# Sixteen resident weight units and twelve head rotations whose sums are made by accumulating transfers

## The chip, the cores and the metric

One NeuronCore of a Trainium2 chip runs the whole kernel in one launch. The metric is the device time of that core in microseconds (us). The engines are TensorE (PE in the rows, its weight loads PEld), VectorE (DVE), ScalarE (ACT), GpSimd (POOL) and SyncE (SP), which here only issues transfers.

## What is computed

One decoder layer on x (8 batches of 100 tokens, 1024 wide) with a context of 8 x 722 rows:

```python
# retention, 8 heads, key width 128, value width 256
q, k, v, g = x @ Wq, x @ Wk, x @ Wv, x @ Wg          # q and k get a rotary turn:
x1, x2 = halves of the 128 wide head
rope = concatenate([x1 * cos - x2 * sin, x2 * cos + x1 * sin])
scores = (q * scale) @ k.T * decay                   # causal
o = scores @ v;  o = o * rsqrt(mean(o*o) + eps) * weight * silu(g)
x = layernorm(x + o @ Wo)
# attention over context and tokens, 16 query heads, 4 key/value heads of 128
q, k = rope(rmsnorm(...)), keys and values of the context in front
x = layernorm(x + softmax(q @ k.T) @ v @ wo)         # wo: 2048 x 1024
# feed-forward of width 4096
x = layernorm(x + (silu(x @ gate) * (x @ up)) @ down)
```

All of it is in float32 accuracy. A product a @ b is made as three products of rounded parts, high x high, high x low, low x high, where low = value - high.

## The kernel before

**Layout.** Activations stand with 128 channels on the partitions and the 800 tokens (NT) along the free axis, 1024 channels as KT = 8 tiles. A *weight unit* is 128 output channels of a 1024 x 1024 piece, 128 x 1024 numbers (512 KB). SP loads two units at a time (1024 KB) from HBM into one of the two slots of `RAW`, in the order in which `_pack_weights` laid them out. ACT copies a unit into its rounded high part (`WH`), DVE subtracts it and so makes the low part (`WL`), and TensorE multiplies. `WH` and `WL` hold two units each. A slot of `RAW` is loaded again once the low parts of its two units are made (`weight_stream`, waiting for `c.w_lo`). Every engine runs its own list of instructions in the order of the code; semaphores (`wait_ge`, `then_inc`) tie them.

**Retention (`phase_retention`).** Heads 1 to 6 are alike (`head(i)`, 72.6 us each): three blocks of seven products by a Strassen scheme (`product`), the output projection of the head before (`project_output`, L2362 to L2364), then `scores`, `turn`. On DVE `combine` (L2031) adds partial products into the block's result; product 3 of a block waits for its first one (`u2`). Q and k come out of block 0 in `QKR`. DVE turns them: `rotate_cos` (L2073) writes T1 = QKR * cos, `rotate_sin` (L2078) writes T2 from the other half of the partitions in two instructions of 64 partitions, `rotate_sum` (L2086) makes T1 - T2, ACT copies the high part (`rotated_hi`, L1764), DVE makes the low part (`rotated_lo`, L2090). `add_output` (L2100) adds a projected tile to the residual `R`; tile n of the projection waits for `add_output(n - 2)`.

**Between retention and attention.** The last two heads' projection runs by halves of 400 tokens (HALF), so that the first layernorm (`HalfNorm`: mean, centre L1452, squares L1433, variance, root, refine L1458 to L1463, normal L1470) of one half lies beside the products of the other. DVE also makes here the low parts of the four value units (`values_lo`, L2114, into `VW`).

**The tail (`phase_tail`).** The attention output projection has 16 units. The second eight (from `U_WO1`) are used by halves: all eight units on tokens 0 to 399, then all eight on tokens 400 to 799. Before, they stand twice in the packed weights, are loaded twice and split twice (`split_hi` L93, `split_lo` L99). The feed-forward goes in four chunks. The down projection of the last chunk (`down_by_halves`, L3687 to L3689) has the same pattern: eight units on 400 tokens, then the same eight loaded and split again (`unit_hi` L3775, `unit_lo` L3996) for the other 400, with the last layernorm (`final`) between and behind them. Its variance of half 0 is taken ahead of unit 12 (`take_variance`, L1420). After the last product come the mean, eight centrings, the last squares, two folds (L1355), variance, root, three refining steps and eight `normal`s, and SP stores the result in pairs of tiles.

**GpSimd** sets some constants and is otherwise free.

Of the kernel before, what the change touches and what calls it, by code (L numbers as in the profile page):

```python
# [21 lines left out]
F32 = mybir.dt.float32  # L22
F32R = mybir.dt.float32r
# [39 lines left out]
U_FFN = U_WO1 + 16  # L63
U_END = U_FFN + 24 * CHUNKS + 8
PRODUCTS = 7
ENTRIES = 8 * PRODUCTS + 2 * KT
PAIRS = U_END // 2

# [87 lines left out]
def phase_context(c, nc, sem):  # L156

    with ExitStack() as ctx:
# [1121 lines left out]
        done.k_stored, done.v_stored = k_stored, v_stored  # L1280
        done.K_STORED = [k_stored_by(GROUPS) for _ in range(2)]
# [16 lines left out]
class HalfNorm:  # L1298

    def __init__(self, c, sem_of, name, mean_banks, var_banks, SUM, SQ, Y, Z,  # L1300
                 folded=(0, 0)):
# [4 lines left out]
        self.folded = folded  # L1306
# [5 lines left out]
    @staticmethod  # L1312
    def half(ap, h):
        return ap[:, h * HALF:(h + 1) * HALF]

    @staticmethod
    def tile(x, k, h):
        return x[:, k, h * HALF:(h + 1) * HALF]

    def mean_bank(self, h):  # L1320
        return self.c.PS[:, self.MEAN_BANK[h], 0:HALF]

    def var_bank(self, h):
        return self.c.PS[:, self.VAR_BANK[h], 0:HALF]
# [23 lines left out]
    def add_last_four(self, dve):  # L1348

        for n, (a, b) in enumerate(((4, 5), (6, 7), (4, 6))):  # L1350
# [4 lines left out]
            dve.tensor_tensor(self.SQ[:, a, :], self.SQ[:, a, :], self.SQ[:, b, :],  # L1355
                              ALU.add).then_inc(self.sq_sum, 1)

    def take_last_variance(self, pe):
        for k in range(5):
# [4 lines left out]
            mm = pe.matmul(self.var_bank(1), self.ones[:], self.SQ[:, k, :], start=(k == 0),  # L1364
# [3 lines left out]
    def add_squares(self, dve, h, ks):  # L1368

        for k in ks:  # L1370
# [3 lines left out]
            dve.tensor_tensor(self.SQ[:, 0, :], self.SQ[:, 0, :], self.SQ[:, k, :],  # L1374
                              ALU.add).then_inc(self.sq_sum, 1)

    def add_pairs(self, dve, h):

        for n, (a, b) in enumerate(((0, 1), (2, 3), (4, 5), (6, 7), (0, 2), (4, 6), (0, 4))):
# [4 lines left out]
            dve.tensor_tensor(self.SQ[:, a, :], self.SQ[:, a, :], self.SQ[:, b, :],  # L1384
# [8 lines left out]
    def add_fours(self, dve, h):  # L1393

        adds = ((0, 1), (2, 3), (0, 2), (4, 5), (6, 7), (4, 6))
        for n, (a, b) in enumerate(adds[:self.folded[h]]):
# [4 lines left out]
            dve.tensor_tensor(self.SQ[:, a, :], self.SQ[:, a, :], self.SQ[:, b, :],  # L1401
                              ALU.add).then_inc(self.sq_sum, 1)

    def take_variance_of_fours(self, pe, h):
        parts = (4, 5, 6, 7, 0) if self.folded[h] == 3 else (0, 4)
        for k in parts:
# [6 lines left out]
            mm = pe.matmul(self.var_bank(h), self.ones[:], self.SQ[:, k, :],  # L1413
# [3 lines left out]
    def take_variance(self, pe, h):  # L1417
        if self.folded[h]:
            pe.wait_ge(self.sq_sum, self.folds(h + 1))
            pe.matmul(self.var_bank(h), self.ones[:], self.SQ[:, 0, :], start=True,  # L1420
                      stop=True).then_inc(self.sq_used, 1)
            return
        for k in range(KT):
            pe.wait_ge(self.squared, KT * h + k + 1)
            pe.matmul(self.var_bank(h), self.ones[:], self.SQ[:, k, :], start=(k == 0),
                      stop=(k == KT - 1)).then_inc(self.sq_used, 1)

    def squares(self, act, h, ks):
        for k in ks:
# [3 lines left out]
            act.activation(self.SQ[:, k, :], self.tile(self.c.R, k, h),  # L1433
# [75 lines left out]
def phase_retention(c, nc, sem, before, norm):  # L1509


    with ExitStack() as ctx:
# [33 lines left out]
                 "s_raw", "s_masked", "s_hi", "s_lo", "gated", "o_raw", "o_sq", "o_products", "o_ln",  # L1546
                 "o_rs", "o_normed", "o_hi", "o_lo", "wo_raw", "r_added",
                 "v_kept", "v_turned", "wo_last", "o_scaled", "o_back")
        (turned, roped, qk_hi, qk_lo, v_hi, v_lo, s_raw, s_masked, s_hi, s_lo,
         gated, o_raw, o_sq, o_products, o_ln, o_rs, o_normed, o_hi, o_lo, wo_raw,  # L1550
         r_added, v_kept, v_turned, wo_last, o_scaled, o_back) = (sem("r_" + n) for n in names)

        f_hi, F_HI = before.k_sq, 8 * GROUPS
# [130 lines left out]

        def scalar(act):
# [269 lines left out]
        def vector(dve):  # L1955
# [119 lines left out]
            def rotate_sin(i, n, half):  # L2075

                lo, hi = 64 * half, 64 - 64 * half
                ins = dve.tensor_tensor(  # L2078
                    batches(T2[lo:lo + 64]), batches(QKR[hi:hi + 64, n, :]),
                    c.SIN[hi:hi + 64].unsqueeze(1).broadcast_to([64, B, T]), ALU.mult)  # L2080
                if half:
                    ins.then_inc(turned, 1)
# [28 lines left out]
            def values_lo(v):  # L2111
                u = U_V + v
                dve.wait_ge(c.w_hi, u + 1)
                dve.tensor_tensor(c.VW[:, v, 1, :], raw_unit(c, u), c.VW[:, v, 0, :].bitcast(F32),  # L2114
                                  ALU.subtract).then_inc(c.w_lo, 1)

# [16 lines left out]
            def mask_scores(i):  # L2133
                dve.wait_ge(s_raw, i + 1)
# [55 lines left out]
            def head(i):  # L2190
# [38 lines left out]
                product_lo(i, 1, 4)  # L2229
                mix(i, 1, 3)  # L2230
                combine(i, 1, "u2")
                rotate_sin(i, 0, 0)
                product_lo(i, 1, 5)
                rotate_sin(i, 0, 1)
# [3 lines left out]
                rotate_sum(i, 0)  # L2238
                output_entry_lo(i, 0)
                rotated_lo(i, 0)  # L2240
                rotate_cos(i, 1)
                output_entry_lo(i, 1)
                rotate_sin(i, 1, 0)
                combine(i, 1, "c21")
                output_entry_lo(i, 2)
                rotate_sin(i, 1, 1)
# [3 lines left out]
                rotate_sum(i, 1)  # L2250
                output_entry_lo(i, 3)
                add_output(1, i)
                rotated_lo(i, 1)
                add_output(2, i)
                mix(i, 2, 0)
# [77 lines left out]
            for n in range(KT):  # L2333
                add_last(0, n)
                if n == 2 or n == 5:
                    values_lo(n // 3)
# [7 lines left out]
            values_lo(2)  # L2344
            values_lo(3)
# [278 lines left out]
        return sync, scalar, vector, tensor, r_added  # L2624


def phase_heads(c, nc, sem, before, norm, r_added):
# [4 lines left out]
    with ExitStack() as ctx:  # L2632
# [217 lines left out]
        def vector(dve, first_queries, first_maxima):  # L2850
# [30 lines left out]
            copy_value(0)  # L2881
            split_lo(c, dve, U_V + 4)
# [461 lines left out]
def phase_tail(c, nc, sem_of, attention):  # L3344
# [4 lines left out]
    with ExitStack() as ctx:  # L3349
# [5 lines left out]
        def below(words, *tiles):  # L3355

            with ExitStack() as room:
                out = []
                for n, (gap, *shape) in enumerate(tiles):
                    if gap:  # L3360
                        room.enter_context(nc.sbuf_tensor(f"{words}_gap{n}", [P, gap], F32))
                    out.append(room.enter_context(nc.sbuf_tensor(f"{words}{n}", [P, *shape], F32)))
# [4 lines left out]
        f_sum, f_y, f_z, f_sq, ones = below("t_fn", (2 * FLAT + 2 * SIDE, NT), (0, NT), (0, NT),  # L3367
                                            (0, KT, HALF), (0, P))
# [1020 lines left out]
```

## Time and profile before

| | us |
|---|---|
| median of 3 runs | 2636.43 (2636.38 to 2636.45) |
| the profiled execution | 2636.99 |
| its span, first to last instruction | 2635.2 |
| TensorE busy | 2598.2 |
| VectorE busy | 1858.9 |
| ScalarE busy | 1214.2 |

The span is what the rows below divide up; 1.8 us lie around it. A row of a timeline gives start and duration in us; matmuls overlap, so that the distance from one start to the next is what one costs. A bracket at the end of a row is the idle time of the engine ahead of it and what ended it.

### The profile page before, as it was taken

Reading aid. Unit: us, or ns where it says so; the run is one execution under the profiler, and the core shown is the slowest. Engines: PE = TensorE matmul, PEld = TensorE weight load, DVE = VectorE, ACT = ScalarE, POOL = GpSimd, SP = SyncE. Lnnn points to the kernel's source line nnn. Section 1 sums busy time; section 2 is a strip of 40 time slices with the busy share of each in tenths; the row PEclk is TensorE's granted clock in tenths of the full one; section 3 lists DMA queues with packets and bytes.
Section 4 is the critical chain, followed back from the end, with each engine's and each line's share of the span. In section 5 each row is a group of like instructions: output and inputs, shape, how many; then the busy total and the mean of one; then the engine's idle time right before and its main releaser. Section 6 shows DMA issues by size and latency. Waiting matters only on the chain.

```text
span 2635.2 us, 41744 instructions
## 1 busy us (share of the span) xinstructions
PE 2598.2 (99%) x16328; PEld 2465.1 (94%) x16328; DVE 1858.9 (71%) x2546; ACT 1214.2 (46%) x2059; POOL 0.8 (0%) x9
## 2 busy tenths in 40 slices
PE   9999999999999999999999999999999999999997
PEld 9999999989999998998889999899998999999997
DVE  7777776687777774867788888737963763763767
ACT  6555555554444443344466666524431431431432
POOL 0000000000000000000000000000000000000000
PEclk9999999999999999999999999999999999999999
DMA  5444435411111121144156666323121221211122
GB/s 196 160 145 160 153 132 182 141 60 54 50 65 51 63 78 60 53 108 96 68 144 173 173 173 173 96 78 121 40 80 48 66 79 59 70 65 64 65 96 98
DMA packets 137421, 266.16 MB, mean 101 GB/s; under 512 B 24756, under 2 KB 98988, under 8 KB 123308
## 3 DMA queue, kind: packets, MB, share of 16 engines
q1 hardware_dynamic: 137260, 263.92, 31.9%
q8 instruction: 113, 1.85, 0.3%
q14 instruction: 48, 0.39, 0.0%
HBM read 206.63 MB, written 57.26 MB: 100 GB/s over the span
## 4 chain that ended last, share of the span: by engine, by line
PE 86%; DVE 9%; issue 2%; ACT 1%; DMA 0%; DVEq 0%; SPq 0%; ACTq 0%
PE PS L3632 6%; PE PS L3630 6%; PE PS L3634 6%; PE PS L3127 5%; PE PS L135 4%; PE PS L133 4%; PE PS L134 4%; PE PS L3140 3%; PE PS L1167 3%; PE PS L1169 3%; PE PS L1171 3%; PE PS L1130 3%; PE PS L1132 3%; PE PS L1134 3%; PE PS L3667 3%; PE PS L3666 3%
## 5 line engine op out<-in xcount | busy, mean ns | idle before, releaser
L3758 ACT ACTIVATE WH<-RAW 128x512 fp32r<-128x512 f32 x180 | 113.4, 631 | 222.5 <-PE PS L3634 120.2
L133 PE MATMUL PS<-XH,WH 128*128 128x512 f32 (+1 forms) x592 | 204.2, 345 | 1.0 <-DVE WL L99 1.0
L135 PE MATMUL PS<-XH,WL 128*128 128x512 f32 (+1 forms) x592 | 204.4, 345 | 0.0
L3991 DVE TENSOR_TENSOR WL<-RAW,WH 128x512 fp32r<-128x512 f32 x196 | 134.7, 688 | 58.5 <-ACT WH L3758 55.2
L134 PE MATMUL PS<-XL,WH 128*128 128x512 f32 (+1 forms) x496 | 170.1, 343 | 0.0
L3632 PE MATMUL PS<-XL,WH 128*128 128x400 f32 x480 | 166.0, 346 | 0.0
L3630 PE MATMUL PS<-XH,WH 128*128 128x400 f32 x480 | 164.8, 343 | 0.8 <-issue 0.6
L3634 PE MATMUL PS<-XH,WL 128*128 128x400 f32 x480 | 165.1, 344 | 0.0
L3299 DVE TENSOR_TENSOR XL<-PS,XH 128x400 fp32r<-128x400 f32 (+2 forms) x224 | 122.6, 571 | 56.4 <-ACT XH L3232 51.6
L3232 ACT ACTIVATE XH<-PS 128x400 fp32r<-128x400 f32 (+2 forms) x224 | 106.4, 507 | 96.1 <-PE PS L3140 96.0
L93 ACT ACTIVATE WH<-RAW 128x1024 fp32r<-128x1024 f32 x55 | 58.3, 1060 | 199.1 <-PE PS L135 147.5
L99 DVE TENSOR_TENSOR WL<-RAW,WH 128x1024 fp32r<-128x1024 f32 x56 | 68.6, 1225 | 106.1 <-ACT WH L93 101.8
L3667 PE MATMUL PS<-t_ROOM,WL 128*128 128x512 f32 (+1 forms) x384 | 132.5, 345 | 0.0
L3666 PE MATMUL PS<-t_ROOM,WH 128*128 128x512 f32 (+1 forms) x384 | 131.7, 343 | 0.0
L3665 PE MATMUL PS<-t_ROOM,WH 128*128 128x512 f32 (+1 forms) x384 | 131.6, 343 | 0.0
L3280 DVE TENSOR_REDUCE a_LOW<-PS 100x1 f32<-100x824 f32 x128 | 129.7, 1014 | 2.6
L1706 ACT ACTIVATE WH<-RAW 128x512 fp32r<-128x512 f32 x132 | 81.3, 631 | 106.9 <-DVE RAW L2005 56.5
L3630 PE MATMUL PS<-t_ROOM,WH 128*128 128x400 f32 x360 | 124.4, 346 | 0.4 <-issue 0.3
L1167 PE MATMUL PS<-WALL,WH 128*128 128x256 f32 x448 | 124.4, 278 | 0.0
L1169 PE MATMUL PS<-WALL,WL 128*128 128x256 f32 x448 | 124.3, 277 | 0.0
L1171 PE MATMUL PS<-WALL,WH 128*128 128x256 f32 x448 | 124.2, 277 | 0.0
L3632 PE MATMUL PS<-t_ROOM,WH 128*128 128x400 f32 x360 | 124.1, 345 | 0.0
(517 smaller groups left out, 8315.2 us busy)
## 6 DMA issues: line engine op xcount, KB each, us to landing
RAW<-weights_dram SPq DMA_DIRECT2D x108, 1024.0 KB, 4.8
values_scratch<-VS SPq DMA_DIRECT2D x44, 512.0 KB
a_KHL<-keys_scratch SPq DMA_DIRECT2D x32, 411.0 KB, 5.1
RAW<-context_dram SPq DMA_DIRECT2D x6, 2048.0 KB, 8.4
XH<-values_scratch SPq DMA_DIRECT2D x16, 640.0 KB
XL<-values_scratch SPq DMA_DIRECT2D x16, 640.0 KB
R<-context_dram SPq DMA_DIRECT2D x4, 2048.0 KB, 9.1
keys_scratch<-KS SPq DMA_DIRECT2D x16, 512.0 KB, 3.8
```

The costliest lines, as they stand in the source:

```text
L133: pe.matmul(out, wh, xh[:, k, cols], start=(k == 0), stop=False)
L134: pe.matmul(out, wh, xl[:, k, cols], start=False, stop=False)
L135: mm = pe.matmul(out, wl, xh[:, k, cols], start=False, stop=(k == KT - 1))
L1167: pe.matmul(out, hi[:, k, cols], wh, start=(opens and t + k == 0), stop=False, skip_group_check=True)
L1169: pe.matmul(out, lo[:, k, cols], wh, start=False, stop=False, skip_group_check=True)
L1171: mm = pe.matmul(out, hi[:, k, cols], wl, start=False, stop=(k == QUAD - 1), skip_group_check=True)
L3630: pe.matmul(out, wh, high[:, k, :], start=(OPENS[p] and k == 0), stop=False, skip_group_check=True)
L3632: pe.matmul(out, wh, low[:, k, :], start=False, stop=False, skip_group_check=True)
L3634: mm = pe.matmul(out, wl, high[:, k, :], start=False, stop=(k == QUAD - 1), skip_group_check=True)
L3666: pe.matmul(out, wh, HL[:, k, cols], start=False, stop=False)
L3667: mm = pe.matmul(out, wl, HH[:, k, cols], start=False, stop=(i == KT - 1))
L3991: dve.tensor_tensor(ring[1][:, e % RING, :], src, ring[0][:, e % RING, :].bitcast(F32), ALU.subtract).then_inc(f_lo, 1)
```

## The change

1. The second eight projection units, and the eight down units of the last chunk, are loaded once and stay for both passes (`kept_weights`, `last_down`). Units 0 and 1 of each lie in `WH` and `WL` as before, and the other twelve in space that is free then (`kept_parts`; `XH` and `XL`). The packed weights lose 16 units. On these units ACT and DVE split nothing a second time.
2. The low parts of those twelve units and of the four value units are no longer made by DVE. ACT writes the negated high part into the low part's place (`minus_hi`), and GpSimd issues a transfer that adds the raw unit to it (`add_raw`), waits for its landing, and then raises the semaphore that DVE raised before.
3. In heads 1 to 6 the rotation's sum is made by two accumulating transfers of 64 partitions, T1 += T2 of the other half. `rotate_sin` becomes one instruction over 128 partitions that writes the negated product. The places in the order change with it.
4. The last down projection and the last layernorm are split into 512 and 288 tokens (PARTS) in place of 400 and 400. The variance of part 0 is taken ahead of unit 13, and its `normal`s stand later.

```diff
+def minus_hi(c, act, lo, raw):
+    act.activation(lo, raw, ACT.Copy, scale=-1.0).then_inc(c.minus, 1)
+
+def add_raw(c, pool, n, lo, raw, landed, by=1):
+    pool.wait_ge(c.minus, c.MINUS + n + 1)
+    pool.dma_start(lo, raw, accum_op=ALU.add).then_inc(c.sum_in, 16)
+    pool.wait_ge(c.sum_in, 16 * (ROPE_SUMS + n + 1))
+    pool.sem_inc(landed, by)
...
+        def gpsimd(pool):
+            sums = 0
+            for i in range(1, END):
+                for n in range(2):
+                    pool.wait_ge(turned, 2 * i + (n + 1))
+                    for lo in (0, 64):
+                        sums += 1
+                        pool.dma_start(T1[lo:lo + 64], T2[64 - lo:128 - lo],
+                                       accum_op=ALU.add).then_inc(rope_in, 16)
+                    pool.wait_ge(rope_in, 16 * sums)
+                    pool.sem_inc(roped, 1)
+            pool.wait_ge(c.w_lo, U_V)
+            for v in range(KV_N):
+                add_raw(c, pool, v, c.VW[:, v, 1, :], raw_unit(c, U_V + v), c.w_lo)
...
                 act.activation(c.VW[:, v, 0, :], raw_unit(c, u), ACT.Copy).then_inc(c.w_hi, 1)
+                minus_hi(c, act, c.VW[:, v, 1, :], raw_unit(c, u))
...
-            def rotate_sum(i, n):
-                dve.wait_ge(turned, 2 * i + (n + 1))
-                dve.tensor_tensor(T1, T1, T2, ALU.subtract).then_inc(roped, 1)
+            def rotate_sin(i, n):
+                dve.scalar_tensor_tensor(
+                    out=batches(T2), in0=batches(QKR[:, n, :]), scalar=-1.0,
+                    in1=c.SIN[:].unsqueeze(1).broadcast_to([P, B, T]), op0=ALU.mult,
+                    op1=ALU.mult).then_inc(turned, 1)
...
         def gpsimd(pool):
+            pool.wait_ge(c.w_lo, U_WO1 + 2)
+            for n in range(KEPT_UNITS):
+                add_raw(c, pool, KV_N + n, kept_weights(n + 2)[1], raw_unit(c, U_WO1 + n + 2), c.w_lo)
             pool.wait_ge(f_done, PER * LAST + 56)
             pool.memset(ones[:], 1.0 / D).then_inc(ones_made, 1)
+            pool.wait_ge(f_lo, PER * LAST + 60)
+            for n in range(KEPT_UNITS):
+                add_raw(c, pool, KV_N + KEPT_UNITS + n, last_down(n + 2)[1], down_raw(n + 2), f_lo, 2)
...
+            def kept_hi(n):
+                u = U_WO1 + n
+                act.wait_ge(c.raw[(u // 2) % 2], 16 * (u // 4 + 1))
+                act.wait_ge(c.unit_done, U_WO1 - U_RET)
+                act.activation(kept_weights(n)[0], raw_unit(c, u), ACT.Copy).then_inc(c.w_hi, 1)
+                minus_hi(c, act, kept_weights(n)[1], raw_unit(c, u))
...
             for i in range(2 * KT):
-                split_hi(c, act, U_WO1 + i + 2)
+                if i + 2 < KT:
+                    kept_hi(i + 2)
+                if i == KT + 1 or i == KT + 2:
+                    first_hi(i - KT - 1)
...
-                split_lo(c, dve, U_WO1 + i + 2)
+                if i == KT + 1:
+                    dve.wait_ge(c.w_lo, U_FFN)
+                if i == KT + 1 or i == KT + 2:
+                    unit_low(U_FFN + i - KT - 1, first_weights(i - KT - 1))
...
-                act.wait_ge(f_done, PER * t + (56 + 2 * n - 2))
+                act.wait_ge(f_done, PER * t + (56 if t == LAST else 56 + 2 * n - 2))
...
-                    if n == KT + 4:
+                    if n == KT + 5:
                         final.take_variance(pe, 0)
...
             final.add_last_four(dve)
+            for k in range(5, KT):
+                final.normal(dve, 0, k)
             final.refine(dve, 1)
```

What this moves, at three places. **DVE in head 4**, from the cosine of the first rotation to its low part (L1973 and L2014 are `product_lo`, low parts of weight quarters; T is T1 or T2, U2 and W belong to `combine`). Before:

```order
L2073 TENSOR_TENSOR T<-QKR,COS 128x800
L1973 TENSOR_TENSOR WL<-RAW,WH 128x512
L2005 TENSOR_TENSOR RAW<-RAW 128x512
L2031 TENSOR_TENSOR W<-U,PS 128x400
L2078 TENSOR_TENSOR T<-QKR,SIN 64x800
L1973 TENSOR_TENSOR WL<-RAW,WH 128x512
L2078 TENSOR_TENSOR T<-QKR,SIN 64x800
L2031 TENSOR_TENSOR W<-W,PS 128x400 x2
L1973 TENSOR_TENSOR WL<-RAW,WH 128x512
L2086 TENSOR_TENSOR T<-T 128x800
L1973 TENSOR_TENSOR WL<-RAW,WH 128x512
L2090 TENSOR_TENSOR QK<-T,QK 128x800
```

Now:

```order
L2114 TENSOR_TENSOR T<-QKR,COS 128x800
L2014 TENSOR_TENSOR WL<-RAW,WH 128x512
L2118 SCALAR_TENSOR_TENSOR T<-QKR,SIN 128x800
L2046 TENSOR_TENSOR RAW<-RAW 128x512
L2072 TENSOR_TENSOR W<-U,PS 128x400
L2014 TENSOR_TENSOR WL<-RAW,WH 128x512
L2072 TENSOR_TENSOR W<-W,PS 128x400 x2
L2014 TENSOR_TENSOR WL<-RAW,WH 128x512 x2
L2125 TENSOR_TENSOR QK<-T,QK 128x800
```

Two instructions of about 800 columns are gone, and the sine now stands ahead of `W<-U,PS`, the combination `u2` that product 3 waits for.

**ACT at the second eight projection units.** Before, one high part for each use, interleaved with the layernorm; L93 stands for each split:

```order
L93 ACTIVATE WH<-RAW 128x1024 x8
L1433 ACTIVATE t_an<-R 128x400 x4
L93 ACTIVATE WH<-RAW 128x1024
L1433 ACTIVATE t_an<-R 128x400 x4
L93 ACTIVATE WH<-RAW 128x1024 x3
```

Now six pairs of high part (L3781) and negated high part (L107) come in a row, of which two are shown, and then the squares of the layernorm:

```order
L3781 ACTIVATE t_wo_0<-RAW 128x1024
L107 ACTIVATE t_wo_1<-RAW 128x1024
L3781 ACTIVATE t_wo_0<-RAW 128x1024
L107 ACTIVATE t_wo_1<-RAW 128x1024
...
L1455 ACTIVATE t_an<-R 128x400 x8
L3788 ACTIVATE WH<-RAW 128x1024 x2
```

The splits of the second pass are gone, and the first two feed-forward units follow the squares.

**GpSimd over the whole program** (`T<-T` are the rotations, `t_wo_...` the kept projection units, `XL` the kept down units):

```order
L1717 DMA T<-T 64x800 x24
L113 DMA VW<-RAW 128x1024 x4
L113 DMA t_wo_1<-RAW 128x1024 x4
L113 DMA t_wo_0<-RAW 128x1024
L113 DMA t_wo_1<-RAW 128x1024
L3509 MEMSET t_fn 128x128
L113 DMA XL<-RAW 128x1024 x6
```

Before, only the memset was there. Of the sixteen transfers of whole units none starts before the one ahead of it has landed.

## Rows read from the trace of the kernel before

**Rows 1.** Page: engine totals (busy us, share of the span, instructions); span and clock.

```profile
PE 2598.2 (99%) x16328; PEld 2465.1 (94%) x16328; DVE 1858.9 (71%) x2546; ACT 1214.2 (46%) x2059; POOL 0.8 (0%) x9
core 0: 2635.2 us, clock 0.998
```

**Rows 2.** Waits of PE: who ended them, us in total, times, longest.

```profile
PE PS L2362 <- DVE R L2100: 2.2, 6, 0.4
...
PE PS L1338 <- DVE n_SUM L1333: 1.1, 2, 0.8
...
PE PS L1420 <- DVE t_fn L1374: 1.0, 1, 1.0
PE PS L1420 <- DVE t_an L1374: 0.9, 1, 0.9
PE PS L1488 <- DVE XL L1475: 0.9, 2, 0.7
```

**Rows 3.** Timeline of DVE in head 4: start, us, instruction, shapes.

```profile
790.21 0.68 DVE L1973 TENSOR_TENSOR WL<-RAW,WH 128x512 fp32r<-128x512 f32 x1
...
791.54 0.56 DVE L2031 TENSOR_TENSOR W<-U,PS 128x400 f32<-128x400 f32 x1
792.14 0.99 DVE L2078 TENSOR_TENSOR T<-QKR,SIN 64x800 f32<-64x800 f32 x1
...
796.64 0.99 DVE L2086 TENSOR_TENSOR T<-T 128x800 f32<-128x800 f32 x1
...
798.57 0.99 DVE L2090 TENSOR_TENSOR QK<-T,QK 128x800 fp32r<-128x800 f32 x1 [0.34 <-ACT QK L1764]
```

**Rows 4.** Timeline of PE in head 4, at product 3 and in the projection.

```profile
791.85 0.34 PE L2505 MATMUL PS<-SIDE,WL 128*128 128x400 f32 x1
792.16 0.46 PE L2501 MATMUL PS<-SIDE,WH 128*128 128x400 f32 x1
...
807.71 0.29 PE L2364 MATMUL PS<-VHL,WL 128*128 128x288 f32 x1
808.37 0.50 PE L2362 MATMUL PS<-VHL,WH 128*128 128x512 f32 x1 [0.37 <-DVE R L2100]
```

**Rows 5.** Page: DMA issues, KB each, median us from issue to landing.

```profile
RAW<-weights_dram SPq DMA_DIRECT2D x108, 1024.0 KB, 4.8
...
keys_scratch<-KS SPq DMA_DIRECT2D x16, 512.0 KB, 3.8
...
out_dram<-R SPq DMA_DIRECT2D x8, 400.0 KB, 2.6
...
keys_scratch<-KS SPq DMA_DIRECT2D x4, 26.0 KB, 2.4
```

**Rows 6.** Timeline at the second projection units: ACT's split, DVE's additions.

```profile
1760.67 1.06 ACT L93 ACTIVATE WH<-RAW 128x1024 fp32r<-128x1024 f32 x1 [6.88 <-PE PS L135]
...
1765.69 0.57 DVE L3923 TENSOR_TENSOR R<-R,PS 128x400 f32<-128x400 f32 x1 [0.90 <-PE PS L1490]
...
1791.78 0.57 DVE L3923 TENSOR_TENSOR R<-R,PS 128x400 f32<-128x400 f32 x1 [1.97 <-PE PS L1490]
```

**Rows 7.** Timeline at the last down projection: ACT, then DVE's first addition.

```profile
2544.38 1.62 ACT L3789 ACTIVATE t_ROOM<-t_G 128x800 fp32r<-128x800 f32 x2
...
2548.41 0.57 DVE L4070 TENSOR_TENSOR R<-R,PS 128x400 f32<-128x400 f32 x1 [0.98 <-PE PS L3689]
```

**Rows 8.** Timeline of DVE ahead of the first layernorm's refining steps.

```profile
1082.41 2.35 DVE L2114 TENSOR_TENSOR VW<-RAW,VW 128x1024 fp32r<-128x1024 f32 x2
```

**Rows 9.** Chain of work behind the last product: start, us, what.

```profile
2618.01 3.95 DVE R L1452 x8
...
2623.88 0.92 PE PS L1364 x2
...
2626.03 0.64 DVE t_fn L1458
...
2628.97 2.91 DVE R L1470 x6
```

More of the change, by code:

```diff
@@ L1280, in phase_context @@
         done.k_stored, done.v_stored = k_stored, v_stored
+        c.again, c.AGAIN = wk_mix, 4
+        done.wv_mix = wv_mix
+        c.minus, c.MINUS = wv_hi, 8
         done.K_STORED = [k_stored_by(GROUPS) for _ in range(2)]
@@ L1310, in __init__, with width, half, tile @@
              "normed", "hi", "lo"))
[L1312 to L1318, printed above, removed]
+    def width(self, h):
+        return self.parts[h][1] - self.parts[h][0]
+    def half(self, ap, h):
+        return ap[:, slice(*self.parts[h])]
+    def tile(self, x, k, h):
+        return x[:, k, slice(*self.parts[h])]
+    def square(self, k, h):
+        return self.SQ[:, k, 0:self.width(h)]
     def mean_bank(self, h):
-        return self.c.PS[:, self.MEAN_BANK[h], 0:HALF]
+        return self.c.PS[:, self.MEAN_BANK[h], 0:self.width(h)]
     def var_bank(self, h):
-        return self.c.PS[:, self.VAR_BANK[h], 0:HALF]
+        return self.c.PS[:, self.VAR_BANK[h], 0:self.width(h)]
     def add_row(self, dve, h, n, added, count):
@@ L1363, in take_last_variance @@
                 pe.wait_ge(self.sq_sum, self.folds(1) + 3)
-            mm = pe.matmul(self.var_bank(1), self.ones[:], self.SQ[:, k, :], start=(k == 0),
+            mm = pe.matmul(self.var_bank(1), self.ones[:], self.square(k, 1), start=(k == 0),
                            stop=(k == 4))
@@ L1419, in take_variance @@
             pe.wait_ge(self.sq_sum, self.folds(h + 1))
-            pe.matmul(self.var_bank(h), self.ones[:], self.SQ[:, 0, :], start=True,
+            pe.matmul(self.var_bank(h), self.ones[:], self.square(0, h), start=True,
                       stop=True).then_inc(self.sq_used, 1)
@@ L1424, in take_variance @@
             pe.wait_ge(self.squared, KT * h + k + 1)
-            pe.matmul(self.var_bank(h), self.ones[:], self.SQ[:, k, :], start=(k == 0),
+            pe.matmul(self.var_bank(h), self.ones[:], self.square(k, h), start=(k == 0),
                       stop=(k == KT - 1)).then_inc(self.sq_used, 1)
@@ L3433, in first_weights, with kept_weights @@
             return hh[:, at], hl[:, at]
+        def kept_weights(n):
+            if n < 2:
+                return c.WH[:, n, :], c.WL[:, n, :]
+            return tuple(x[:] for x in kept_parts[n - 2])
         def raw_count(t, pair):
@@ L3472, in chunk @@
             def chunk(t, first, last):
-                for i in range(4 if first else 0, 16 if last else 12):
+                for i in range(4 if first else 0, 12):
                     load(t, i)
@@ L3685, in down_by_halves @@
                         w = slice(k * P, (k + 1) * P)
-                        wh, wl = c.WH[:, n % 2, w], c.WL[:, n % 2, w]
+                        wh, wl = high[:, w], low[:, w]
                         pe.matmul(out, wh, HH[:, k, cols], start=(i == 0), stop=False)
@@ L3857, in chunk @@
                         hidden_hi(t, 3, 0)
[L3858 removed]
+                    if n + 2 < KT:
                         unit_hi(t, n + 2)
@@ L4167, in chunk @@
                             final.add_squares(dve, 0, range(4, KT))
-                        if n == KT + 3:
+                        if n == KT + 5:
                             final.refine(dve, 0)
-                        if n > KT + 3:
-                            for k in range(2 * (n - KT - 4), 2 * (n - KT - 3)):
-                                final.normal(dve, 0, k)
+                        for k in {KT + 6: range(3), KT + 7: range(3, 5)}.get(n, ()):
+                            final.normal(dve, 0, k)
                 else:
@@ L4188, in vector @@
             final.add_last_four(dve)
+            for k in range(5, KT):
+                final.normal(dve, 0, k)
             final.refine(dve, 1)
@@ L4345, in _pack_weights @@
     put(*(_unit(a["L0_xattn_wq"], h * HD) for h in range(QH_N)))
-    for g in (0, 1, 1):
+    for g in range(2):
         put(*(_unit(a["L0_xattn_wo"][g * D:(g + 1) * D], n * P) for n in range(KT)))
@@ L4352, in _pack_weights @@
                 put(*(_unit(w, t * D + n * P) for n in (k, k + 1)))
-        for _ in range(2 if t == CHUNKS - 1 else 1):
-            put(*(_unit(down[t * D:(t + 1) * D], n * P) for n in range(KT)))
+        put(*(_unit(down[t * D:(t + 1) * D], n * P) for n in range(KT)))
     return out
```

149 lines of the change are left out of this document (79 added, 70 removed).

## The prediction

> **What bounds the kernel now.** Read the engine totals first: TensorE is busy for 2598.2 of 2635.2 us at full clock [rows 1]. The change leaves the columns of its matmuls as they are in sum, so it can win only in the 37 us in which TensorE stands still, and DVE and ACT time saved elsewhere is worth nothing. Next, the waits of PE [rows 2] say where those 37 us lie and who ended them: six waits on `add_output` in the heads, two on the first layernorm's sum, one variance at the attention layernorm and one at the last one, two on low parts at the start of the feed-forward. Last, the chain behind the last product [rows 9]: from the first centring at 2618.01 us to the span's end nothing is multiplied but norms, 17.2 us, all of it serial. These places, and the new waits on GpSimd's transfers, are all that has to be priced.
>
> **Part 1: rotations.** At each rotation DVE loses one instruction of 64 x 800 and the sum, each 0.99 us [rows 3]. That looks like a cure for the projection's waits: PE starts at 808.37 in place of 807.84 (807.71 and 0.13 for 288 columns) [rows 4], 0.53 us, and about 0.3 us more go at tile 2 and in restarts, some 0.84 us a head. But the sine, now 128 x 800 in one piece, stands ahead of `u2`. Before, `u2` starts at 791.54 and product 3 starts at 792.16, right behind it, 0.13 us late [rows 3, 4]. A sine of 800 columns takes 0.9 to 1.0 us, so product 3 starts near 793.05 and PE loses 0.9 us a head. Sum: 6 x (0.9 - 0.84), about +0.3 us. I take +0.3; the bounds are -1 (the sine overlaps better) and +1.
>
> The transfers must land in time. The sine ends near 791.8; the low part of the rotation (L2090) stood at 798.57 and is followed by two whole instructions fewer before `add_output(0)` and `(1)`. Counting DVE's list forward from it, its start may slip to about 800.8 before tile 2 or 3 waits; minus 0.9 us for ACT's copy and 0.1 for the semaphore, the landing may take 8 us. The nearest rows for two transfers of 200 KB in flight together are the 400 KB one, 2.6 us, and the 1024 KB one, 4.8 us [rows 5]. So this is hidden, with 3 us to spare. What it hides behind is `combine` and `product_lo` of block 1.
>
> **Part 2: value units.** Two of the four low parts, 2.35 us, stand right ahead of the refining steps [rows 8]. Without them these wait for ACT's root instead, which now comes some 0.6 us late since two negated copies of about 1 us are queued ahead of it: net 0.4 us earlier. The other two stood ahead of the first mean. So of PE's 1.1 us on the sum [rows 2] I take back 0.7 us (0.3 to 1.1).
>
> **Part 3: the kept projection units.** Here a new wait arises. ACT makes unit 1's high part at 1760.67 in 1.06 us, then unit 2's high and negated part, about 1 us each, so GpSimd can start at 1763.65 [rows 6]. From there six transfers run strictly one behind the other; with a cycle of C us (wait, issue, landing, increment) unit 7 is ready at 1763.65 + 6C. PE goes through a unit of 400 columns in 4.35 us ([rows 6]: from 1765.69 to 1791.78 in six units), and needs unit 7 at 1791.6. So PE stands still for 6C - 27.95 us if C is over 4.66. What queues behind it: DVE's additions and all of the layernorm of that half.
>
> How long is C? No row shows an accumulating transfer, nor one issued by GpSimd. From [rows 5]: a fixed part near 2.4 (26 KB), 512 KB in 3.8, so 1.4 us for each 512 KB moved. Lower bound 3.8 (as a plain transfer); upper 2.4 + 3 x 1.4 = 6.6 (two reads and a write without overlap). An accumulation reads 1024 KB and the row that reads as much takes 4.8. I take that and 0.1 for GpSimd's wait and increment: C = 4.9, so +1.45 us (0 at the lower, +11.65 at the upper bound).
>
> The Trainium skill gives a price of its own: "DMA: Bandwidth & Descriptors", section "Anatomy of one DMA — SWDGE (gpsimd) path", fits a GpSimd-issued transfer as 2.0 us plus bytes at 436 GB/s, and "Collectives: The Full Stack", section "The bandwidth ceiling", says that an adding transfer is slower only because it reads two sources. By these an estimate for 512 KB read twice is 4.4 us, no stall at all, and 1.45 us less in the sum. No row here tests either.
>
> Against it, what the freed DVE gives: the variance of that layernorm (L1420 on t_an) [rows 2] still waits, since two feed-forward low parts stay ahead of the squares' sum; 0.2 of its 0.9 us goes. The 0.9 us at the feed-forward's start (L1488) [rows 2] goes nearly whole, as the split ahead of it, some 1.2 us [rows 8], is gone. Together -1.1 us (-0.5 to -1.6).
>
> **Part 4: the last down projection.** GpSimd can start when unit 2's negated part is there: ACT is free at 2544.38 + 1.62 = 2546.0 [rows 7], and two copies later it is 2548.1. A unit of 512 columns takes PE about 5.5 us ([rows 6]: a unit of 512 and 288 takes 8.71), and the pass begins at 2543.8 (the first addition, 2548.41 [rows 7], less one unit of 4.35 and 0.26 for the way to DVE, my estimate). Seven units later, at 2582.2, unit 7 is needed, and the stall is 6C - 34.1: nothing at 4.9, 5.5 us at 6.6. Columns sum to the same.
>
> The variance ahead of unit 13 no longer waits: in the 3.2 us units of 288 columns DVE, freed of its splits of 1.2 us, has the squares summed some 2.5 us earlier than PE asks. That gives 1.1 us; the two norm matmuls of 512 columns take back 0.35: -0.75. Behind the last product a DVE instruction of 288 columns is shorter than one of 400 by 0.12 us ([rows 3]: 0.56, 0.68 and 0.99 us for 400, 512 and 800). The centrings wait for two late `normal`s, -0.15 only; centrings -0.95; squares, two folds, variance, root -0.75; refining -0.35; `normal`s -0.95 [rows 9]. The three late `normal`s of 512 columns, some 1.8 us, just fit beside variance and root, 2623.88 to 2626.03 [rows 9]. Sum -3.9 us (-3.0 to -4.6).
>
> **The sum.** 2635.2 + 0.3 - 0.7 + 1.45 - 1.1 - 3.9 = 2631.25 of span; with 1.8 around it 2633.0, and less 0.56, by which the profiled run lies over the median, 2632.5. That is 0.15% under before. A measurement of this kernel can tell about 0.2%, 5.3 us, from no change.
>
> **Rivals.**
> - *The cycle is at or under 4.66.* Then nothing stalls and 5.4 us stay: 2631.0, down to 2629.1 with the other terms at their good ends. For it: 400 KB land in 2.6 us. The skill's estimate above leads here.
> - *The cycle is over 6.05: GpSimd's chain becomes the bound.* At 6.0 both stalls together are 8.05 + 1.9 us, 2641.0; at 6.6 it is 17.15 us, 2648.2; at 7 some 2653. It decides from C = 5.56, where 6C - 27.95 has used up the gain of 5.4, and is slower by more than 0.2% (2641.7) from 6.05 on, where the second stall adds to the first. For it: the issue on GpSimd is software of unknown price, sixteen sums are serial, weight loads of 1024 KB share the engines. Against it: PE needs the units one by one, and only the later ones are late.
> - *The rotation's landing is late.* If two half transfers take over 8 us, ACT and DVE stand in front of `rotated_lo` in all six heads, 1 us for each us: at 10, 12 us in all, 2644. The rows near it give half of that.
> - *The change gives nothing at the end.* If squares or the late `normal`s take the centrings' place on the chain, part 4 gives 2 us: 2634.4.
>
> **How the numbers follow.** Forecast case with the last rival: 0.46. Cycle under the cadence: 0.27. Cycle over 6.05: 0.20. Late rotation: 0.03. Cycle between 5.56 and 6.05: 0.04, no change that can be told. The first rival lies at the edge of 0.2%; with it go a few hundredths where other terms are better than taken: faster 0.29, same 0.48, slower 0.23. The range reaches from 2629.0, all terms good and no stall, to 2648.0, the upper bound of the cycle.
>
> **What would show it.** Right: the transfers into t_wo in issue-to-landing near 4.8; PE waiting 1 to 2 us on GpSimd at 1790 and not at 2580; PE in each head idle ahead of product 3 by about 0.9 us and no wait on L2100's successor; the chain from last product to last store about 3 us shorter; no wait of 1 us at the last variance. Wrong: waits of PE on GpSimd that grow from unit to unit, or DVE idle in front of L2125 while PE stands. A change of the granted clock would upset all of it.

## The result, and the profile after

| | before | after |
|---|---|---|
| median, us | 2636.45 (2636.38 to 2637.51, 7 runs) | 2646.11 (2643.66 to 2646.43, 7 runs) |
| ratio, 95% interval | | 1.0034 (1.0025 to 1.0043) |
| profiled execution, its span | 2636.99, 2635.2 | 2646.11, 2644.3 |

The change makes the kernel 0.34% slower, 9.7 us, where 4 us of gain were forecast. The head of the page, to be read beside [rows 1]:

```profile
PE 2598.6 (98%) x16328; PEld 2460.9 (93%) x16328; DVE 1796.6 (68%) x2490; ACT 1211.8 (46%) x2059; POOL 34.7 (1%) x49
```

TensorE has as many matmuls as before and is busy as long. VectorE is relieved of 62 us, ScalarE of 2, and the span is 9.1 us longer. The waits of PE, with the longest in the last column:

```profile
PE PS L1510 <- POOLq L115: 9.2, 4, 4.2
...
PE PS L2522 <- DVE W L2072: 5.9, 6, 2.1
PE PS L3744 <- POOLq L115: 1.7, 2, 1.3
...
PE PS L1525 <- DVE XL L1497: 1.6, 2, 1.1
...
PE PS L1442 <- DVE t_an L1396: 0.7, 1, 0.7
PE PS L1360 <- DVE n_SUM L1355: 0.6, 1, 0.6
```

L1510 is the second eight projection units, L3744 the last down projection, L2522 a head's product: gone are the waits on `add_output` and on the last variance of half 0 [rows 2], new are the two on GpSimd's increment, L115. Of the six waits at L2522 five are new, of 0.76 us each; the longest, 2.1 us in the first head, was there before with 1.3.

**Where the 9.1 us arise.** Both programs have the same 16328 matmuls. Taking the n-th of one from the n-th of the other gives by how much the changed kernel is behind at each point:

| stretch | behind at its end, us | change in it |
|---|---|---|
| up to the last Strassen head (0.26 of it ahead of the first) | -0.45 | -0.45 |
| end of retention, first layernorm | -1.55 | -1.1 |
| kept projection units, first pass | +12.85 | +14.4 |
| second pass, layernorm, start of feed-forward | +10.83 | -2.0 |
| feed-forward | +10.79 | -0.04 |
| last down projection | +12.54 | +1.75 |
| behind the last product | +9.1 | -3.4 |

(The 0.26 us of the first row were lost ahead of the first head, where the traces of these kernels differ by up to 0.8 us.) One term is far from its forecast, the first pass over the kept projection units; the others lie within about 2 us of theirs. GpSimd's transfers in it (start, us of the issue alone; the bracket is the idle time ahead and what ended it):

```profile
1762.59 0.86 POOL L113 DMA_DIRECT2D t_wo<-RAW  x1 [676.07 <-ACT t_wo L107]
1770.55 0.86 POOL L113 DMA_DIRECT2D t_wo<-RAW  x1 [7.11 <-DMA t_wo<-RAW]
1775.63 0.89 POOL L113 DMA_DIRECT2D t_wo<-RAW  x1 [4.21 <-DMA t_wo<-RAW]
1784.61 0.88 POOL L113 DMA_DIRECT2D t_wo<-RAW  x1 [8.09 <-DMA t_wo<-RAW]
1789.82 0.87 POOL L113 DMA_DIRECT2D t_wo<-RAW  x1 [4.33 <-DMA t_wo<-RAW]
1798.83 0.90 POOL L113 DMA_DIRECT2D t_wo<-RAW  x1 [8.14 <-DMA t_wo<-RAW]
```

The five cycles are 7.96, 5.08, 8.98, 5.21 and 9.01 us. And SP's weight loads of 1024 KB in the same stretch:

```profile
1761.59 0.33 SPq L82 DMA_DIRECT2D RAW<-weights_dram  x1
...
1775.27 0.33 SPq L82 DMA_DIRECT2D RAW<-weights_dram  x1
1789.37 0.33 SPq L82 DMA_DIRECT2D RAW<-weights_dram  x1
```

Each long transfer, at 1762.59, 1775.63 and 1789.82, follows a load by 0.4 to 1.0 us; no load begins beside the short ones. That is no accident: the landing of a pair's second transfer raises `w_lo`, and this releases SP's next load and GpSimd's next transfer alike (the first load was released by the same semaphore, there from VectorE's low part of unit 1). The long transfers are held back at their start. These are the queues' packets, MB and share of the 16 engines in the first 4.3 us of the second transfer, which runs alone, and of the third:

```profile
q0 software_dynamic: 144, 0.52, 64.4%
...
q1 hardware_dynamic: 119, 0.97, 82.3%
```

The second has by then moved all its packets, the third (1775.7 to 1779.9) none; only the load's are on the engines. Its first comes 4.4 us after its issue begins, in place of 1.4, when the load is nearly through. The page shows the issues (KB each, median us to landing); the long and the short ones together make the median:

```profile
T<-T POOLq DMA_DIRECT2D x24, 200.0 KB, 3.2
t_wo<-RAW POOLq DMA_DIRECT2D x6, 512.0 KB, 5.9
XL<-RAW POOLq DMA_DIRECT2D x6, 512.0 KB, 4.6
VW<-RAW POOLq DMA_DIRECT2D x4, 512.0 KB, 4.5
```

**The clock.** Table by stretch, of which the column PEclk, behind the five engines, is the granted clock:

```profile
1780.00:1785.00 5.00, 1.00 (x3) 1.00 (x4) 0.99 (x2) 3.53 (x4) 0.39 (x1) 0.74 0.57 118
1785.00:1790.00 5.00, 5.00 (x19) 4.96 (x18) 0.00 (x0) 0.37 (x1) 0.68 (x2) 0.58 0.55 105
```

TensorE stood idle for 4.2 us, and then ran at the lower of its two levels, 1.2 GHz, for most of the next 5 us. In the timeline:

```profile
1784.00 0.70 PE L1510 MATMUL PS<-XL,t_wo 128*128 128x400 f32 x1 [4.18 <-POOLq L115]
1784.50 0.54 PE L1511 MATMUL PS<-t_ROOM,t_wo 128*128 128x400 f32 x1
1784.83 0.54 PE L1512 MATMUL PS<-XL,t_wo 128*128 128x400 f32 x1
```

Two starts are 0.33 us apart, against 0.18 for 400 columns at 2.4 GHz. This costs 2.5 us here, which the next wait swallows, and 1.74 us behind the last stall, at 1798.34, where nothing swallows them.

### The profile page after: what moved, and what is told of

Read it like the earlier page. It is cut to its first block, busy times and chain, and to the rows that moved or that the text cites. A ratio compares the mean times of both kernels' runs of the same rounds, so it can differ in the third digit from the quotient of the medians.

```text
span 2644.3 us, 41693 instructions
## 1 busy us (share of the span) xinstructions
PE 2598.6 (98%) x16328; PEld 2460.9 (93%) x16328; DVE 1796.6 (68%) x2490; ACT 1211.8 (46%) x2059; POOL 34.7 (1%) x49
## 4 chain that ended last, share of the span: by engine, by line
PE 89%; DVE 5%; DMA 2%; issue 2%; ACT 1%; DVEq 0%; SPq 0%; ACTq 0%; POOLq 0%
PE PS L3687 6%; PE PS L3685 6%; PE PS L3689 6%; PE PS L3149 5%; PE PS L150 4%; PE PS L148 4%; PE PS L149 4%; PE PS L3162 3%; PE PS L1182 3%; PE PS L1184 3%; PE PS L1186 3%; PE PS L1145 3%; PE PS L1147 3%; PE PS L1149 3%; PE PS L3723 3%; PE PS L3722 3%
## 5 line engine op out<-in xcount | busy, mean ns | idle before, releaser
L3689 PE MATMUL PS<-t_ROOM,WL 128*128 128x400 f32 x360 | 124.1, 345 | 0.0
L148 PEld LDWEIGHTS PS<-XH,WH 128*128 128x128 f32 x592 | 111.4, 188 | 12.6 <-issue 1.2
```

The lines of the kernel that those rows point to most:

```text
L148: pe.matmul(out, wh, xh[:, k, cols], start=(k == 0), stop=False)
L3689: mm = pe.matmul(out, wl, high[:, k, :], start=False, stop=(k == QUAD - 1), skip_group_check=True)
```

## The experiments

Rows and sums of these kernels are compared with the changed kernel, 2646.1 us, or with each other; before, measured beside them, was 2637.2 us in the first four and 2637.05 us in the last four. Beside the changed kernel it had been 2636.45, so that a difference to 2646.1 is uncertain by some 0.8 us.

**kept_by_dve** gives the low parts of the kept units back to VectorE.

```diff
 def kept_hi(n):
...
                 act.activation(kept_weights(n)[0], raw_unit(c, u), ACT.Copy).then_inc(c.w_hi, 1)
-                minus_hi(c, act, kept_weights(n)[1], raw_unit(c, u))
...
                 attn.add_row(dve, h, n, added, 4 + 8 + i + 1)
+                if i + 2 < KT:
+                    unit_low(U_WO1 + i + 2, kept_weights(i + 2))
...
                         add_half(t, n)
+                        if n + 2 < KT:
+                            unit_lo(t, n + 2)
```

> The changed kernel, but VectorE makes the low parts of the twelve kept units as it did before the change (one subtraction of 128 x 1024 behind each addition); no negated copies for them, and no transfer of GpSimd. The rotations, the value units, the loading once and the 512/288 split stay. Theory A (the accumulating transfer of a kept unit takes 5.1 us alone and 9.0 us when a weight load of 1024 KB runs beside it; PE's stalls, and half-speed matmuls behind them, are nothing but its result): the 14.4 us that PE loses between 1758 and 1809 us go, and 2.4 us of the down projection too, 2646.1 - 16.8 = 2629.3 us; granted clock 1.00 all through the kept projection. Rival B (the clock falls, and loads are slow, for a reason that has nothing to do with GpSimd): the stalls go, 10 + 2 us, the 4.5 us of half clock stay, 2634.

Measured: 2629.86 us (2629.29 to 2630.78), ratio to before 0.9973 (0.9962 to 0.9983). All waits on GpSimd are gone, and so is the low clock (same columns as above):

```profile
1780.00:1785.00 5.00, 5.00 (x29) 5.00 (x28) 2.28 (x3) 0.00 (x0) 0.00 (x0) 1.00 0.63 213
1785.00:1790.00 5.00, 5.00 (x30) 5.00 (x29) 2.29 (x3) 0.00 (x0) 0.00 (x0) 1.00 0.14 21
```

So 16.2 us, more than the whole loss, come from making these low parts by transfer. Theory A holds, B falls: the clock fell only behind the stalls. VectorE has the time: it is busy for 20.5 of the 40 us from 1760 on, with this work in it. Summing the units by transfer isn't worth having. Loading them once seems to be, though no run undoes it alone: in this trace the two stretches that it bears on, from the second pass to the start of the feed-forward and the last down projection, are 2.1 and 0.4 us shorter than before, the second with the split in it.

**load_held** takes one load away from the transfers' side.

```diff
-            weight_stream(c, sp, U_WO // 2 + 2, (U_FFN - U_WO) // 4 + 1)
+            weight_stream(c, sp, U_WO // 2 + 2, (U_FFN - U_WO) // 4 - 1)
+            for pair in range(U_FFN // 2, U_FFN // 2 + 4):
+                sp.wait_ge(c.w_lo, max(2 * pair - 2, U_FFN))
+                sp.dma_start(c.RAW[:, pair % 2, :], c.weights[pair]).then_inc(c.raw[pair % 2], 16)
```

> The changed kernel, but SP issues the first load of feed-forward weights only when all six transfers of the kept projection units have landed, so that nothing runs beside the fifth and sixth. Theory A (collision with the weight load): the fifth cycle is 5.1 us in place of 9.0, the wait of 3.1 us ahead of unit 7 goes and with it some 1.4 us of half clock behind it: 2641.6 us. The first and third cycle, beside which a load still runs, stay at 8 and 9 us. Rival C (long and short alternate by themselves, by destination, by the queue or by the chip's descriptors): the fifth cycle stays at 9.0, and the time at 2646.

Measured: 2641.05 us, lowest 2640.19 (one of eleven executions took 5052 us, which I can't explain; the median does not feel it). GpSimd, third to sixth transfer:

```profile
1776.32 0.89 POOL L113 DMA_DIRECT2D t_wo<-RAW  x1 [4.21 <-DMA t_wo<-RAW]
1784.99 0.88 POOL L113 DMA_DIRECT2D t_wo<-RAW  x1 [7.78 <-DMA t_wo<-RAW]
1790.16 0.87 POOL L113 DMA_DIRECT2D t_wo<-RAW  x1 [4.29 <-DMA t_wo<-RAW]
1796.78 0.90 POOL L113 DMA_DIRECT2D t_wo<-RAW  x1 [5.75 <-DMA t_wo<-RAW]
```

The third cycle, with its load, is 8.67 us (8.98 in the changed kernel), and the fifth, without, fell from 9.01 to 6.62. This is the collision, and rival C falls; but 5.1 was expected. The queues' shares (packets, MB, share of the 16 engines) in the fifth transfer, from 1790.2 to 1796.2, show what is beside it:

```profile
q0 software_dynamic: 144, 0.52, 47.5%
q8 instruction: 1, 0.02, 1.5%
```

One packet of 16 KB from the instruction queue runs among the 144 of this transfer, and in the sixth, which takes 5 us again, there is none. The fifth down unit of the changed kernel, 6.47 us with no load beside it, has one too. In all these runs the adding transfers without a load land 4.5 to 4.7 us after their issue begins, but 5.5 to 6.0 in the four cases in which such a packet falls among theirs, and 4.76 where it just misses them (here, fifth down unit, cycle 5.34). That the packet is the cause of the 1.5 us rests on these coincidences; no run removes it.

**plain_copy** moves the same number of bytes to the same places without adding; its kept and value low parts hold raw weights, so part of the computation is another one.

```diff
-    pool.dma_start(lo, raw, accum_op=ALU.add).then_inc(c.sum_in, 16)
+    pool.dma_start(lo, raw.bitcast(lo.dtype)).then_inc(c.sum_in, 16)
```

> The changed kernel, but the sixteen transfers of whole units copy the raw unit over the negated high part in place of adding it, so those low parts hold the raw weights and the output is another one; number, size, queue and order of the transfers are the same. Theory F (adding is what is dear: a second source is read): a lone cycle falls from 5.1 us to about 4.0 and one beside a load from 9.0 to under 6, stalls nearly gone, about 2634 us. Theory A in its plain form (any transfer of GpSimd's queue yields to a load of 1024 KB): lone near 4.5, beside a load still 8 or more, about 2643 us.

Measured: 2636.55 us in one execution.

```profile
1769.23 0.54 POOL L113 DMA_DIRECT2D t_wo<-RAW  x1 [6.13 <-DMA t_wo<-RAW]
1772.67 0.54 POOL L113 DMA_DIRECT2D t_wo<-RAW  x1 [2.90 <-DMA t_wo<-RAW]
1780.13 0.54 POOL L113 DMA_DIRECT2D t_wo<-RAW  x1 [6.92 <-DMA t_wo<-RAW]
```

A cycle alone is 3.44 us in place of 5.08, one beside a load 6.7 to 7.9 in place of 8.0 to 9.0. So both are true in part: adding costs 1.1 to 1.6 us of each cycle (0.3 of it in the issue, 0.54 against 0.86), and a load beside it costs 3 to 4.5 us whether the transfer adds or not. The time lies between the two expectations.

**sine_behind** tests the stall that part 1 of the change made in each head.

```diff
-                rotate_sin(i, 0)
                 mix(i, 1, 3)
                 combine(i, 1, "u2")
+                rotate_sin(i, 0)
```

> The changed kernel with one instruction of VectorE moved in heads 1 to 6: the sine of the first rotation stands behind mix 3 and the combination u2, not ahead of them. Nothing is left out. Theory D (product 3 of block 1 waits 0.93 us in each head for nothing but this sine): 6 x 0.93 = 5.6 us less, 2640.5 us, PE's waits on L2072 gone. Rival E (the rotation is 1.2 us later and turns into another wait, at the low part of the rotation and then add_output): at most 1 us less, 2645.

Measured: 2653.6 us (2652.92 to 2654.84), 7.5 us slower than the changed kernel. Both theories miss. The six waits for the sine are gone, as D says, but PE now waits for `add_output` in head 2 (3.8 us) and in head 6 (4.3 us), and for 0.8 us in head 5, where a rotation lands late. In head 6 GpSimd, SP, and ScalarE's copy of the rotation:

```profile
941.46 0.81 POOL L1717 DMA_DIRECT2D T<-T  x1 [60.52 <-DVE T L2118]
944.80 0.83 POOL L1717 DMA_DIRECT2D T<-T  x1 [2.54 <-issue]
...
944.69 0.33 SPq L1678 DMA_DIRECT2D RAW<-weights_dram  x1
...
951.41 0.87 ACT L1805 ACTIVATE QK<-T 128x800 fp32r<-128x800 f32 x1 [7.96 <-POOLq L1720]
```

Two things come together. Between the two halves GpSimd stands still for 2.5 us with nothing to wait for; the changed kernel has this gap too, at the 8th and at the 22nd of the 24 rotation transfers and nowhere else between halves. And here the second half meets a weight load. From the sine's end to the copy, a rotation takes 4.9 to 5.5 us, with the gap 6.8 (changed kernel), with gap and load 10.3. The late one of head 5 takes 6.8 without the gap. A load follows it closely, but so it does others that take 5.3; what it has beside them is a packet of the instruction queue among its own, like the one of 6.9 in head 3 of the changed kernel. Moved by one instruction, the sine brought the transfer onto the load.

**loads_wait** takes these loads out of the way. It is kept_by_dve with the sine behind `u2`, as in sine_behind, and these waits of SP (the edit of the sine is not shown again):

```diff
                 sp.wait_ge(f_lo, F_LO + PER * (i - 1) + 14)
+                sp.wait_ge(roped, 2 * i + 1)
                 load_pair(pair_of(i, 3))
                 sp.wait_ge(f_lo, F_LO + PER * (i - 1) + 18)
+                sp.wait_ge(roped, 2 * i + 2)
```

> VectorE makes the low parts of the kept units, and the sine stands behind u2 as in sine_behind; besides, SP issues a head's fourth load of weights only when the first rotation's two transfers have landed, and the next head's first load when the second's have. Nothing is left out. Theory G (in sine_behind the rotation was late in heads 2 and 6 alone because a weight load was issued beside its second half: 10.3 us in place of 6.8): now no rotation takes over 7 us, PE does not wait for add_output, and the 5.6 us of product 3 are won whole: 2629.9 - 5.6 = 2624.3 us. Rival H (they were late from something else, or the loads, now up to 4 us later, are missed by ScalarE and so by PE): over 2628, and over 2636 if the rotations stay as late as they were.

Measured: 2626.45 us (2626.38 to 2626.75), ratio to before 0.996 (0.9947 to 0.9974). This is the fastest of the kernels here, 10.6 us under before. ScalarE's copy in head 6:

```profile
941.02 0.87 ACT L1807 ACTIVATE QK<-T 128x800 fp32r<-128x800 f32 x1 [4.53 <-POOLq L1722]
```

The sine ends at 934.20, so 6.8 us, and no rotation takes longer: theory G. The later loads keep nobody waiting. Of the 5.6 us, 3.4 came: heads 2 and 6, those with the gap, still lose 0.6 and 1.1 us at the projection, and 0.14 us a head stays ahead of product 3, as before the change.

**rotation_by_dve** undoes the rotations, on top of kept_by_dve.

```diff
-            for i in range(1, END):
-                for n in range(2):
-                    pool.wait_ge(turned, 2 * i + (n + 1))
...
+            def rotate_sum(i, n):
+                dve.wait_ge(turned, 2 * i + (n + 1))
+                dve.tensor_tensor(T1, T1, T2, ALU.subtract).then_inc(roped, 1)
```

> As kept_by_dve, and the rotations as before the change: cosine, two sines of 64 partitions and the sum on VectorE, at their old places; GpSimd sums only the four value units. By the two traces a head loses 0.94 us ahead of product 3 now and lost 1.07 us in three places before, so part 3 of the change is worth 6 x 0.13 us: expected 2630.7 us. Rival: if the transfers cost something that the waits do not show (weight loads held up), the kernel gets faster without them, under 2629.9.

Measured: 2630.12 us (2629.74 to 2630.93), 0.3 us over kept_by_dve, which the medians can't tell from nothing. Matmul by matmul, this kernel loses 0.8 us to kept_by_dve over the six heads in the two traces, 0.27 of which it had gained ahead of the first. As it stands in the change, the rotation by transfer gives under 1 us; freed of the sine's place and of the loads it gives 3.7 (2630.1 against 2626.45).

**kept_400** undoes the split into 512 and 288, on top of kept_by_dve; the places of the variance and of the late `normal`s stay as changed.

```diff
-        final = HalfNorm(c, sem, "fn_", (1, 5), (3, 7), f_sum[:], f_sq, f_y[:], f_z[:],
-                         (7, 0), PARTS)
+        final = HalfNorm(c, sem, "fn_", (1, 5), (3, 7), f_sum[:], f_sq, f_y[:], f_z[:],
+                         (7, 0), ((0, 400), (400, NT)))
...
-                    cols = slice(*PARTS[h])
+                    cols = slice(h * HALF, (h + 1) * HALF)
                     high, low = last_down(n % KT)
```

> As kept_by_dve, but the last down projection and the last layernorm are split into 400 and 400 tokens again. My sum put the 512/288 split at 3.2 us behind the last product, less 0.35 us for wider norm matmuls: expected 2629.9 + 3.0 = 2632.9 us. Rival (what ended the wait of the last variance was the missing splits, and the shorter second part gives little, because the late normals take its place): within 1 us of 2629.9.

Measured: 2632.72 us (2631.99 to 2633.91), 2.9 us over kept_by_dve. The split is worth what it was priced at.

**two_in_flight** asks whether the serial waiting is what costs.

```diff
-            for n in range(KEPT_UNITS):
-                add_raw(c, pool, KV_N + n, kept_weights(n + 2)[1], raw_unit(c, U_WO1 + n + 2), c.w_lo)
+            for n in range(0, KEPT_UNITS, 2):
+                for m in (n, n + 1):
+                    pool.wait_ge(c.minus, c.MINUS + KV_N + m + 1)
+                    pool.dma_start(kept_weights(m + 2)[1], raw_unit(c, U_WO1 + m + 2),
+                                   accum_op=ALU.add).then_inc(c.sum_in, 16)
+                pool.wait_ge(c.sum_in, 16 * (ROPE_SUMS + KV_N + n + 2))
+                pool.sem_inc(c.w_lo, 2)
```

> The changed kernel, but GpSimd issues the transfers of two kept projection units one behind the other and waits for both. One at a time, a pair takes 13.0 to 14.3 us (one beside a load, one alone). If the long one is held up by the load for a fixed time and the rest is latency, a pair takes about 10.5 us and unit 7 is there 8 us earlier: about 2638 us. If the three transfers only share what the DMA engines can move, a pair takes 13 us as before, and the time is 2646 or more, since the first of a pair is released with the second.

Measured: 2645.52 us in one execution.

```profile
1762.09 0.86 POOL L3509 DMA_DIRECT2D t_wo<-RAW  x1 [676.05 <-ACT t_wo L107]
1770.03 0.86 POOL L3509 DMA_DIRECT2D t_wo<-RAW  x1 [7.08 <-ACT t_wo L107]
1775.11 0.89 POOL L3509 DMA_DIRECT2D t_wo<-RAW  x1 [4.21 <-DMA t_wo<-RAW]
1783.34 0.88 POOL L3509 DMA_DIRECT2D t_wo<-RAW  x1 [7.34 <-ACT t_wo L107]
1788.52 1.80 POOL L3509 DMA_DIRECT2D t_wo<-RAW  x2 [4.30 <-DMA t_wo<-RAW]
```

The edit did not do what it says for two pairs of three. The second issue came 7.94 and 8.23 us after the first, though the code waits only for ScalarE, whose negated part was ready at 1763.4 in the first pair; the bracket names it for want of another. Only the last pair went out together, and it took 11.1 us from first issue to both landings (1799.60), with a load beside it, against 13.0 for the first pair and some 14 one at a time. So the question was only answered for one pair, which speaks for latency. In the other two the second issue began 0.20 to 0.25 us after the first transfer had landed (at 1769.78 and 1783.14), as if GpSimd had waited for it; what holds it back stays open.

## Why the prediction was wrong

**Bounds and method.** That TensorE bounds the kernel, that only its 37 idle us can be won, and that GpSimd's chain is the danger, all held. The formula of part 3 came close too: with the mean cycle measured, 36.24 / 5 = 7.25 us, 6C - 27.95 gives 15.5 us, and 14.4 were lost. In part this is luck. The formula has PE waiting for unit 7, but the sixth transfer was a short one and nobody waited for it; the 14.4 us are a delay of 12.7 at unit 6 and 1.74 of low clock behind it, which no term held.

**The step that failed: "How long is C?"** I took 4.9 us. A cycle alone is 5.08 us, so this price was good, but by two errors that cancel: 4.5 us from the issue's start to the landing, where I took 4.8, and 0.55 from there to the next issue, where I took 0.1. The estimate beside it held: the Trainium skill's rule for a transfer by GpSimd ("DMA: Bandwidth & Descriptors", section "Anatomy of one DMA — SWDGE (gpsimd) path"), with both sources counted, gave 4.4 us, and the trace shows these 4.5 us for a transfer alone. But I applied my price to six transfers of which three run beside a weight load. That loads "share the engines" stood among the rival's reasons without a price, and it could have been placed: `weight_stream` waits for `w_lo`, the very semaphore that the transfer raises. A chain that releases its own competitor collides at every load, not now and then: the third, fifth and, in the down projection, third transfer did. The slower rival (cycle over 6.05) came true, with a mean of 7.25 us in the projection and 6.2 us in the down projection, and I gave it 0.20. Both passes lost time where I had 1.45 and 0 us in the sum.

**A second step: where the stall lies.** I expected one wait near unit 7. There were four, at units 2, 3, 4 and 6, since the first transfer was already a long one; and between them TensorE ran at 1.2 GHz, which no term held. Of that only 1.74 us count.

**The other terms.**

| term | forecast | measured | how it compares |
|---|---|---|---|
| heads | +0.3 | -0.45 | product 3 starts 0.79 us later in each head (forecast 0.9), the projection gives back 0.93 (0.84): -0.7; the trace had lost 0.26 ahead of the first |
| value units | -0.7 | -1.1 | at the good end of the bounds; no run undoes this alone |
| second pass, start of feed-forward | -1.1 | -2.0 | -1.2 at the feed-forward's start, where the wait of 0.9 is gone with its restarts; -0.4 around the variance, whose wait fell from 0.9 to 0.7; -0.3 in the feed-forward's first chunk |
| down projection, stalls | 0 | +2.15 | cycles 5.37, 5.09, 8.77, 5.36, 6.47; the long one follows a load by 0.5 us |
| down projection, variance | -0.75 | -0.4 | -1.1 around the last variance of half 0, whose wait is gone; +0.7 in the units' own products, which no term held: 288 columns take 3.20 us, where their share of 8.71, which is twice the 4.35 of [rows 6], is 3.14 |
| behind the last product | -3.15 | -3.4 | below |

The chain behind the last product, to be set beside [rows 9]:

```profile
2629.25 1.20 DVE R L1492 x2
2630.45 2.93 DVE R L1474 x8
2633.40 0.45 ACT t_fn L1455
...
2634.97 0.74 PE PS L1386 x2
...
2636.74 0.53 DVE t_fn L1480
...
2639.11 2.21 DVE R L1492 x6
```

Eight centrings went from 3.95 to 2.93 us and six `normal`s from 2.91 to 2.21; the two late `normal`s ahead of the centrings are the price foreseen, and the three others hide beside variance and root. kept_400 confirms the term by itself: 2.9 us.

**The rotation's landing** was bounded at 8 us; in the changed kernel none takes more than 6.9, so that rival rightly had little. But its reason, "3 us to spare" from transfers alone, was as blind to loads as part 3: sine_behind went over it.

## What to carry to other kernels

Price a new transfer together with the one that the same semaphore releases: here a transfer of 512 KB took 5.1 us alone and 9 us each time the buffer it freed was loaded again beside it. An engine that waits for each landing in turn makes latency into throughput, so before work is moved from an engine that is off the critical path, ask what it costs there: VectorE had the time, and giving the work back to it while keeping the rest of the change won 16 us. When an edit moves a transfer by 1 us, look at what is issued within the next microseconds, as sine_behind and loads_wait show from both sides.

## What the runs showed of the hardware

- An adding transfer of 512 KB issued by GpSimd lands 4.5 us after its issue begins (0.88 us of it the issue), a plain copy 2.9 (0.54). With a load of 1024 KB from HBM issued just ahead of it, the adding one takes 7.3 to 8.4 us, the copy 6.1 to 7.3, and most of this passes before its first packet. The load is held up too: its data were ready some 6 us after the issue in place of 4.8 [rows 5].
- One packet of 16 KB from the instruction queue among an adding transfer's packets went with a landing after 5.5 to 6.0 us in place of 4.5, four times of four; 5.88 and 6.04 in the changed kernel and in load_held.
- GpSimd's queue has pauses that no semaphore explains: 2.5 us ahead of the 8th and the 22nd rotation transfer, in every kernel with 24 of them, and a second issue of 512 KB that began only when the first had landed. In both, the issue begins 0.2 to 0.3 us after the transfer ahead of it lands (the 7th lands at 658.94, the 8th is issued at 659.20). Whether these are one thing wasn't tried.
- Behind 4.2 us of idle time TensorE ran at 1.2 GHz for some 5 us, with its next matmuls 0.33 us apart in place of 0.18. In kept_by_dve, without the idle time, the granted clock is 1.00 throughout this stretch.
